# TensorE multiplies the identity where it waits: an encoder block on one core

## The reference

```python
x = x + 0.5 * ffn(layernorm(x), ...)     # attention, routed experts
x = x + retention(layernorm(x), ...)     # 8 heads, decay mask, gate
x = x + 0.5 * ffn(layernorm(x), ...)     # the same weights again

def ffn(src, ...):                       # 16 heads of 8
    probs = softmax(q @ k.T * 8 ** -0.5) # per batch and head, 256 x 256
    x = layer_norm(src + (probs @ v) @ Wo + bo)
    e = floor(x @ router_w + router_b) mod 4
    h = relu(x @ W1[e] + b1[e]); y = h @ W2[e] + b2[e]
    return layer_norm(x + y)
```

## Time and profile before

| | us |
|---|---|
| median of 3 runs (901.03 to 902.38) | 901.46 |
| the profiled execution | 902.45 |
| its span, first to last instruction | 900.6 |
| TensorE busy | 812.1 (90%) |
| VectorE busy | 740.8 (82%) |
| ScalarE busy | 650.5 (72%) |
| GpSimd busy | 549.7 (61%) |
| mean granted clock of TensorE | 0.962 |

### The profile page before, as it was taken

The page is one execution under the profiler, slowest core; times in us unless marked ns, Lnnn a source line. Parts: engine busy times, 40 slices in busy tenths (PEclk is TensorE's granted clock), DMA queues, the critical chain, the costliest instruction groups (busy, mean ns, idle before and its releaser), DMA issues.

```text
span 900.6 us, 26130 instructions
## 1 busy us (share of the span) xinstructions
PE 812.1 (90%) x8479; PEld 609.2 (68%) x8479; DVE 740.8 (82%) x1841; ACT 650.5 (72%) x1242; POOL 549.7 (61%) x914
## 2 busy tenths in 40 slices
PE   4989999999999699399999988999999999987894
PEld 3656666666665699367878766666666666656894
DVE  4688999999996788569898875789998989967895
ACT  2578888888886488335454554888989889873794
POOL 4126667676755667628676772157676766556676
PEclk9999999999999999789999996999999999999997
DMA  9995699100004688210000000000000000045781
GB/s 281 378 419 143 126 401 415 70 12 24 12 18 145 194 235 275 74 46 2 0 0 0 1 1 1 2 2 14 24 12 23 12 18 18 14 150 171 235 276 49
DMA packets 41813, 96.65 MB, mean 107 GB/s; under 512 B 5224, under 2 KB 25470, under 8 KB 37260
## 3 DMA queue, kind: packets, MB, share of 16 engines
q1 hardware_dynamic: 36236, 83.11, 28.3%
q0 software_dynamic: 5504, 12.63, 3.9%
HBM read 43.64 MB, written 53.13 MB: 107 GB/s over the span
## 4 chain that ended last, share of the span: by engine, by line
PE 57%; DVE 16%; POOL 11%; issue 11%; ACT 2%; DMA 2%; DVEq 0%; SPq 0%; POOLq 0%; ACTq 0%
PE duo L648 10%; PE duo L591 10%; DVE mx L1374 6%; PE duo L584 4%; PE duo L740 3%; PE duo L900 2%; PE duo L585 2%; PE duo L629 2%; PE duo L879 2%; PE duo L567 2%; PE duo L888 2%; PE duo L858 2%; POOL out L1964 2%; PE duo L861 2%; PE duo L631 2%
## 5 line engine op out<-in xcount | busy, mean ns | idle before, releaser
L1374 DVE TENSOR_REDUCE mx<-duo 128x4 fp32r<-128x1024 f32 x256 | 313.5, 1225 | 64.5 <-PE duo L591 57.5
L1064 ACT ACTIVATE probs<-duo 128x1024 f32<-128x1024 f32 x256 | 262.8, 1027 | 42.1 <-PE duo L597 33.8
L591 PE MATMUL duo<-stacks 32*128 32x256 f32 x1024 | 133.4, 339 | 24.7 <-DVE mx L1374 19.9
L648 PE MATMUL duo<-probs,v_st 128*32 128x256 f32 x2048 | 143.1, 399 | 0.5
L597 PE MATMUL duo<-q_st,stacks 32*128 32x256 f32 x1024 | 131.6, 335 | 0.1
L591 PEld LDWEIGHTS duo<-stacks 32*128 32x128 f32 x1024 | 80.3, 191 | 69.0 <-DVE mx L1374 27.0
L1050 ACT ACTIVATE stacks<-duo,small 128x512 fp32r<-128x512 f32 x128 | 88.8, 694 | 9.0 <-PE duo L585 8.4
L584 PE MATMUL duo<-qk_hi,sel_r 128*128 128x256 f32 x256 | 82.5, 342 | 4.1 <-DVE qk_lo L1363 3.5
L648 PEld LDWEIGHTS duo<-probs,v_st 128*32 128x32 f32 x2048 | 54.8, 112 | 42.8 <-issue 4.8
L740 PE MATMUL duo<-w,xs 128*128 x608 | 78.1, 283 | 5.9 <-DVE hidden L1542 2.8
L740 PEld LDWEIGHTS duo<-w,xs 128*128 128x128 f32 x608 | 73.8, 198 | 7.9 <-issue 7.7
(11 more groups left out here) (222 smaller groups left out, 2057.7 us busy)
## 6 DMA issues: line engine op xcount, KB each, us to landing
x_sorted<-ret SPq DMA_DIRECT2D x2, 17476.0 KB, 52.7
wbuf<-w_pack SPq DMA_DIRECT2D x38, 512.0 KB
ret<-x_sorted SPq DMA_DIRECT2D x22, 257.0 KB, 3.1
stacks<-x_sorted SPq DMA_DIRECT2D x12, 257.0 KB, 3.9
wside<-w_pack SPq DMA_DIRECT2D x38, 66.0 KB
w_pack<-wbuf SPq DMA_DIRECT2D x2, 1024.0 KB, 8.4
decay_rows<-prow SPq DMA_DIRECT2D x1, 1536.0 KB
xs<-x_sorted SPq DMA_DIRECT2D x4, 257.0 KB, 3.6
```

Of the source, the lines that this page charges most:

```text
L591: return pe.matmul(score_bank[h % 2][:, t * SEQ:(t + 1) * SEQ], q_st[r:r + 32, g, t * P:(t + 1) * P], k_st[r:r + 32, g, :], start=True, st ...
L648: last = pe.matmul(into[32 * j:32 * j + 32, :], v_st[:, half, t, first:first + VC], probs[:, (g * GH + j) % RING, t, :], start=(t == 0 and ...
L1064: act.activation(probs[:, h % RING:h % RING + 2, :, :], duo_now[:].rearrange("p (n t q) -> p n t q", n=2, t=TT), ACT.Exp, scale=SCALE).the ...
L1374: dve.tensor_reduce(rows, score_duo[:].rearrange("p (n t k) -> p n t k", n=2, t=TT), AX.X, ALU.max, negate=True).then_inc(max_done, 1)
```

## The change

A helper multiplies the identity by itself n times into a PSUM bank that nothing reads at that time; no semaphore is touched. Its calls stand in five kinds of place: behind the bias transpose (2), in setup (1, 6, 4), in slots of batch 0 (1, 6, 2, 4, 4, 3), in slots of batch 16 (5, 3, 2), and ahead of the retention (32, behind a new wait for the last output tile). In a slot the turns stand right behind the score burst. Since those of slots 5 and 6 write into `pv_bank`, which holds the product of L975 until VectorE has read it, the wait for `set_bv` 4 moves from slot 7 of batch 0 to slot 5.

```diff
             turn = {}
+            FIRST_IDLE = ({0: 1, 1: 6, 2: 2, 4: 4, 5: 4, 6: 3}, {1: 5, 5: 3, 6: 2})
+
+            def idle_turns(n, into):
+
+                for _ in range(n):
+                    pe.matmul(into[:, 0:P], ident[:], ident[:], start=True, stop=True)
+
+            idle_turns(2, bank[3])
...
                             score_burst(i, 2 * p, bs, hs, live(i, base), live(bs, base), p if drained(i, base) else None)
+                        if isinstance(i, int) and i == base and p in FIRST_IDLE[base // BATCH]:
+                            idle_turns(FIRST_IDLE[base // BATCH][p], bank[3] if p < 5 else pv_bank)
...
             attend(-1, slots(0, 2))
+            idle_turns(1, bank[3])
             pe.wait_ge(ld_a, 16)
             attend(-1, slots(3, 5))
             pe.wait_ge(set_bv, 2)
             pe.matmul(pv_bank[:, 0:P], bv_rep, wo, start=True, stop=True).then_inc(set_bv, 1)
+            idle_turns(6, bank[3])
             pe.wait_ge(set_act, 1)
             pe.wait_ge(sel_ready, 1)
             attend(-1, slots(6, 7))
+            idle_turns(4, bank[3])
             attend(0, slots(0, 2))
             pe.wait_ge(set_dve, SET_ATT)
-            attend(0, slots(3, 6))
+            attend(0, slots(3, 4))
             pe.wait_ge(set_bv, 4)
+            attend(0, slots(5, 6))
             pe.wait_ge(set_pool, 3)
             attend(0, slots(7, 7))
             iterations(pe, 0, attend)
             experts(0, attend)
+            pe.wait_ge(yo_ready, TILES)
+            idle_turns(32, bank[3])
             retain, attend = retention(), phase(BATCH)
```

## The result

The changed kernel took 896.58 us by median of 20 runs (889.27 to 908.82), the kernel before 901.68 of 20 (894.89 to 920.93). The ratio is 0.9949, 95% interval 0.9925 to 0.9974: 0.5% faster, 4.6 us. Forecast were 13.7. The ratio and its interval leave out executions over 1.5% above the fastest of their kernel, so they are not the quotient of the medians given beside them. The profiled execution has a span of 894.5 us (before 900.6) at a mean clock of 0.974 (before 0.962).

The account below looks back on a forecast made before the run. TensorE at half clock was taken to bound stretches: the start to about 40 us, near 380 us, and batch 16. Phase 0 -7.5, retention -1.7 and batch 16 -4.5 make -13.7, from 901.46 to 887.8 us; range 880.5 to 897.

Parts of the forecast that it names:

- The half clock up to 40 us in setup: Start of the kernel: TensorE runs at 1.2 GHz until about 40 us, though the clock column prints 1.00.
- the price of a turn: One fp32 128x128 identity matmul, two trace records: 0.46 us at the half clock, 0.24 at the full one.
- the 3 to 6 allowed: Clock rise: expected 3 to 6 us into unbroken TensorE work; 4.5 us was read from the trace.
- setup costs nothing to the first burst: Setup up to batch 0's first burst, now at 13.99 us: booked +0.3 us, bounds -0.3 and +2.0.
- the 1.8 us in the first projections: Retention, L858 and L861: 2.07 and 1.72 us at half clock become 1.13 and 0.86, 1.8 together.
- the slots of batch 16, where -4.5 was booked: First batch of the second attention stage: +0.9 for turns, -1.7 earlier rise, -3.7 held clock; bounds +1 and -6.
- the term of batch 0, -5.5: Batch 0 with 20 turns and the clock held: 16.2 us for 21.68, bounds -7.0 to -3.7.
- plus 0.4 for a wait that is late next: Batch 0, behind slot 1: VectorE's packing, reached about 17.9 us, waits for W2's load landing at 18.3; 0.4 us.
- the 16.2 of the forecast: Batch 0's forecast length: a steady batch's 15.84 us plus 0.4 for the wait for W2.
- batch 1, -2.3: Batch 1, no turns: -1.6 in its first two slots, -0.7 for a half chance of no later clock fall.
- the retention, -1.7: 32 turns ahead of the retention: gain 2.0, its start 0.3 later; bounds -2.0 and +0.5.
- this gain is kept: Retention: rotation, heads and first scores start from L861's end, so the 2.0 us gain stays.

Follow-up runs that it names:

- pack_late: The changed kernel with VectorE's packing of the expert weights moved from behind slot 1 of batch 0 to behind slots 3 and 4; 892.59 us, ratio 0.9880 to the kernel before.
- best: The changed kernel with that packing behind slots 3 and 4 of batch 0 and eight more turns in the first retention batches' pauses; 884.16 us, ratio 0.9856.
- ret_hold: The changed kernel with eight more turns in TensorE's pauses of the first retention batches (two, four, two); ratio 0.9926.
- turns_transposed: The changed kernel with every turn issued as two transposes of the identity instead of one matmul; the 64 take 9.3 us, the retention 138.22 us.

## Why the prediction was wrong

**Right.** The half clock up to 40 us in setup, read from durations against a clock column that says 1.00; the price of a turn (32 took 8.78 us, 0.27 each over both clocks); that a multiplied identity lifts the clock (2.8 us into the 32 turns here, up to 5.8 in five other executions, for the 3 to 6 allowed); that setup costs nothing to the first burst (14.31 and 13.52 for 13.99); the 1.8 us in the first projections; the slots of batch 16, where -4.5 was booked and -4.0 is the mean. The measured time is inside the range, by 0.4 us, and the likeliest value is three times too far.

**Wrong: the term of batch 0, -5.5.** It measured -0.5 and -0.1. The step that failed is "plus 0.4 for a wait that is late next: VectorE's packing behind slot 1 needs the load of W2 ... at 18.3". The wait was seen and mis-sized. VectorE came there at 17.9, as forecast, but the load landed at 19.0 instead of 18.3 (issued at 5.2, 13.8 us on its way), so the wait was 1.12 us. Only the idle time at the load was counted, not the 2.15 us of packing behind it, which until then had run while TensorE was slow (18.70 to 20.9, with the burst of slot 2 on its way), and which a shorter slot can't hold. And the idle TensorE behind it was taken to cost its own length, while the clock also came down for 6.8 us behind it. `pack_late` gives the term back: 15.95 us, 0.25 under the 16.2 of the forecast. Over all five executions with the packing early the term is between +0.4 and -2.1, -0.5 in the mean.

**Wrong: batch 1, -2.3.** It measured 0.0 and -0.9. The clock again fell in it (43.08 and 46.9), as the forecast half expected; -1.6 was booked as sure. It did come in the first two slots (3.75 us, 35.72 to 39.47, for 5.49), but behind them TensorE waited 1.45 us for a maximum that VectorE took between its setup work, the clock fell at 43.08, and the batch had 6.8 us of half clock where it had 6.3 before. In `best` and `ret_hold`, where the clock doesn't fall in it, the batch is 1.5 us shorter than before.

**Wrong: the retention, -1.7.** The gain of 2.0 came (1.8 and 0.25), and +3.0 and +1.6 stood against it in the batch behind. The step that failed is "The chain behind it ... starts from L861's end, so this gain is kept". The chain was kept; the clock was not. Before the change it rose at 388.44 and stayed up through the same pauses, of 1.09 and 0.47 us, that came behind it; lifted at 374.17, it fell among them. The forecast followed the clock up to the end of its gain and no further. Why it stays up in one execution and not in another is open: in `turns_transposed`, also lifted early and with open pauses, it stayed, and the stage took 138.22 us. Over the four executions with early turns and open pauses the loss is 1.6 us in the mean, less than the gain.

**Wrong in the base.** Batch 16 was priced against one execution with 39.67 us, the longest of the six seen without turns there. Against their mean of 36.7 the change brings 4.0; the profiles of before and after differ by 6.5. That the booked 4.5 is so near to 4.0 is in part luck: it took away the most that there was to take, from the longest case. A forecast of a gain that hangs on where the clock falls needs more than one execution of the kernel before.

Added up by means of the kernel before and of the two executions of the change, with batch 16 as above: setup and batches 0 and 1 -1, retention +0.3, batch 16 -4.0, some -4.7, and 4.6 were measured. Each of these terms varies by 1 us or more between executions, so that they meet so closely is chance.

## What to carry to other kernels

Before filling TensorE's waits to keep its clock up, ask what else has been hiding behind the slow engine (here a load and 2.15 us of packing); the turns were worth 0.5 us in the mean with it in place and 4.2 us with it moved. Follow the clock past the end of the stretch that is sped up: a clock that rises earlier can fall earlier, and the pauses of the next step may need covering too. And take several profiles of the kernel before when its stages differ by where the clock happens to fall.

## What the runs showed of the hardware that was not expected

The same stream of instructions on TensorE kept the full clock in one execution (but for 2.6 us) and had the half clock for 10 to 20 us in others (32.95 to 39.67 us for two batches). Over the 20 runs of the changed kernel the mean granted clock went from 0.968 to 0.982, and the time fell with it (correlation -0.96, and -0.92 among the faster thirteen), from 908.8 to 889.3 us. In one execution 64 transposes of the identity lifted the clock after 4.4 us, like matmuls of it. After the 32 turns the clock, up at 374.17, fell again at 387.82, although TensorE was busy 10.70 of the 13.65 us between.
